# Sixteen experts on one core: tokens of experts 2 to 15 turned by VectorE and SBUF to SBUF transfers instead of TensorE

## The reference

```python
x = x + attention(layernorm(x), context)        # 16 heads of 16, sigmoid scores, no softmax
x = x + ffn(layernorm(x))

def ffn(h):                                     # b=8, s=512, d=256
    logits = einsum('bsd,ed->bse', h, gate_w)
    scores = softmax(logits, axis=-1).transpose(0, 2, 1)
    topk_w, topk_idx = top_k(scores, 64)        # each expert takes 64 tokens of each batch
    x_tok = take_along_axis(h, topk_idx)        # 16 experts x 8 x 64 rows of 256
    g = einsum('becd,efd->becf', x_tok, Wg)     # f = 512
    u = einsum('becd,efd->becf', x_tok, Wu)
    eo = einsum('becf,edf->becd', gelu(g) * u, Wd) * topk_w
    out = scatter_add(zeros, topk_idx, eo)
    shared = (gelu(h @ Ws_g.T) * (h @ Ws_u.T)) @ Ws_d.T
    return out + shared
```

## Time and profile before

| | |
|---|---|
| median of 3 runs | 1411.19 us (1408.72 to 1411.27) |
| the profiled execution, its own time | 1411.32 us |
| its span in the trace | 1409.5 us |
| instructions | 22306 |
| TensorE's granted clock, mean | 0.992 |
| experts, 0 to 15, in the span | from about 1113 us to the end |

### The profile page before, as it was taken

The page is one execution under the profiler, slowest core; times in us unless marked ns, Lnnn a source line. Parts: engine busy times, 40 slices in busy tenths (PEclk is TensorE's granted clock), DMA queues, the critical chain, the costliest instruction groups (busy, mean ns, idle before and its releaser), DMA issues.

```text
span 1409.5 us, 22306 instructions
## 1 busy us (share of the span) xinstructions
PE 1356.8 (96%) x8906; PEld 780.9 (55%) x8906; DVE 647.5 (46%) x1294; ACT 957.5 (68%) x1073; POOL 210.7 (15%) x173
## 2 busy tenths in 40 slices
PE   4869999999999999999999999999999999999997
PEld 3434444444444344444444443324888888888886
DVE  4334245235325424523532531211658777777773
ACT  3556888888887888888888788998232344444442
POOL 1000000000000000000000000020000236666665
PEclk9998999999999999999999999999999999999999
DMA  6482666387378467548737835732433366666644
GB/s 161 127 154 92 126 124 156 112 136 174 109 122 161 136 117 143 148 108 135 190 100 124 163 107 81 138 121 82 174 120 120 120 194 150 150 149 150 150 105 46
DMA packets 97160, 185.82 MB, mean 132 GB/s; under 512 B 16992, under 2 KB 51296, under 8 KB 97056
## 3 DMA queue, kind: packets, MB, share of 16 engines
q1 hardware_dynamic: 80768, 154.08, 46.2%
q0 software_dynamic: 16000, 29.91, 10.3%
q10 hardware_dynamic: 288, 0.39, 0.2%
HBM read 118.99 MB, written 61.83 MB: 128 GB/s over the span
## 4 chain that ended last, share of the span: by engine, by line
PE 87%; ACT 4%; DVE 3%; DMA 2%; issue 2%; SPq 1%; POOL 0%; POOLq 0%; DVEq 0%
PE acc L1318 24%; PE score L1356 18%; PE score L1294 17%; PE score L1371 9%; PE misc L1209 6%; PE misc L1222 6%; ACT probs L683 4%; PE misc L1245 2%; PE misc L1230 2%; PE misc L1237 1%; DMA key_scr<-key_parts 1%; PE misc L1253 1%; DVE o_sum L863 1%; SPq L391 1%; PE acc L1397 1%
## 5 line engine op out<-in xcount | busy, mean ns | idle before, releaser
L683 ACT ACTIVATE probs<-score 128x1024 f32<-128x1024 f32 (+1 forms) x832 | 789.5, 1043 | 166.8 <-PE score L1294 161.9
L1318 PE MATMUL acc<-probs,values 128*32 128x512 f32 (+1 forms) x3328 | 411.9, 601 | 4.5 <-DVE o_sum L863 3.3
L1294 PE MATMUL score<-queries,keys 48*128 48x512 f32 (+1 forms) x1664 | 315.4, 452 | 4.0 <-DMA keys<-key_parts 3.0
L1294 PEld LDWEIGHTS score<-queries,keys 48*128 48x128 f32 (+1 forms) x1664 | 128.4, 181 | 258.7 <-ACT probs L683 200.6
L692 ACT ACTIVATE gelu<-score 128x512 f32<-128x512 f32 x96 | 57.1, 594 | 198.6 <-PE score L1356 198.5
L1318 PEld LDWEIGHTS acc<-probs,values 128*32 128x32 f32 (+1 forms) x3328 | 83.2, 109 | 184.0 <-issue 144.2
L580 POOL DMA_DIRECT2D ctx_raw<-ctx_t x32 | 23.4, 731 | 759.5 <-DVE ctx_lo L771 758.6
L782 DVE CAST key_parts<-misc 128x512 fp32r<-128x512 f32 (+1 forms) x63 | 36.2, 574 | 209.1 <-PE misc L1209 196.0
L1356 PE MATMUL score<-tok_hi,gu_hi 128*128 128x512 f32 x384 | 119.2, 392 | 0.0
L1356 PE MATMUL score<-tok_lo,gu_hi 128*128 128x512 f32 x384 | 118.6, 390 | 0.0
L1356 PE MATMUL score<-tok_hi,gu_lo 128*128 128x512 f32 x384 | 118.5, 390 | 0.0
(11 more groups left out here) (179 smaller groups left out, 1388.8 us busy)
## 6 DMA issues: line engine op xcount, KB each, us to landing
keys<-key_scr SPq DMA_DIRECT2D x180, 200.2 KB, 8.1
key_scr<-key_parts SPq DMA_DIRECT2D x45, 512.0 KB, 4.5
gu_raw<-w_gu SPq DMA_DIRECT2D x17, 1024.0 KB, 6.5
ctx_raw<-ctx_t POOLq DMA_DIRECT2D x24, 512.0 KB, 4.1
queries<-query_scr SPq DMA_DIRECT2D x180, 64.0 KB, 2.8
d_raw<-w_d SPq DMA_DIRECT2D x17, 512.0 KB, 8.7
query_scr<-query_parts SPq DMA_DIRECT2D x15, 512.0 KB, 5.0
xn<-x SPq DMA_DIRECT2D x8, 512.0 KB, 3.8
```

The lines of the kernel that those rows point to most:

```text
L683: act.activation(probs[0:rows, n % RING, 2 * pair:2 * pair + 2, :], score[k % 3][0:rows, :, :], ACT.Sigmoid, scale=SCALE).then_inc(probs_d ...
L1294: mm = pe.matmul(score[k % 3][0:rows, g, :], keys[quarter % KEY_RING][of, pair, P * st:P * st + rows], queries[half][of, e, pair, :], star ...
L1318: mm = pe.matmul(acc[32 * c:32 * (c + 1), :], values[b % 2][0:rows, st, half, c, :], probs[0:rows, n % RING, c, :], start=(st == 0), stop= ...
```

## The change

The rows of experts 2 to 15 no longer go through TensorE. (`DIRECT_ROWS = 2` experts stay as they were.)

1. `turn(e)` on VectorE: one transpose of the gathered rows in blocks of 32 x 32, into `blocks`, a view of the tile `xn`, which the experts otherwise don't use.
2. `place(e)` on SP: the 16 pairs of a block row and a block column are moved to their partitions by 16 transfers of 32 partitions x 2 x 128 elements, into `tok_raw`, a view of the tile `norm`.
3. `turned_tokens(e)` on VectorE: splits `tok_raw` into `tok_hi` and `tok_lo`, two casts and two subtractions, reading in runs of 32 elements.
4. The multiplication by `add_w` moves from VectorE to ScalarE (`expert_result`), between its two pairs of quarters. VectorE keeps the two small copies (`expert_rows`). For the last expert there is one result and one signal per tile of 128 rows, as before.
5. The orders: gathers are issued up to five experts ahead instead of three, the row lists (`rows_of`) four ahead instead of two, the weight load of set e+3 stands ahead of `place(e+2)` on SP, and weight set 3 and `place(2)` ahead of the store of the last shared result.

```diff
             for n in range(1, B + 1):
 
+                if n == B:
+                    sp.wait_ge(set_split, 4)
+                    load_weights(3, 1)
+                    place(2)
...
+            def place(e):
+
+                sp.wait_ge(turned, e + 1 - DIRECT_ROWS)
+                wait_past(sp, tok_split, e - DIRECT_ROWS)
+                for i in range(BLOCKS):
+                    for j in range(BLOCKS):
+                        sp.dma_start(tok_raw[TURN * j:TURN * (j + 1), :, P * i:P * (i + 1)],
+                                     blocks[TURN * i:TURN * (i + 1), j::BLOCKS, :]).then_inc(placed, 16)
...
-            for s in range(3, SETS):
-                sp.wait_ge(set_split, 2 * s - 2)
-                load_weights(s, s % 2)
+            for e in range(1, E):
+                if e + 3 < SETS:
+                    sp.wait_ge(set_split, 2 * e + 4)
+                    load_weights(e + 3, (e + 1) % 2)
+                if e + 2 < E:
+                    place(e + 2)
...
+                if e >= 2 + DIRECT_ROWS:
+                    pool.wait_ge(turned, e - 1 - DIRECT_ROWS)
+                elif e >= 2:
                     pool.wait_ge(tok_full, TABLES + KC * (e - 1))
...
+            for e in range(5):
+                gather(e, e % 2)
             for e in range(E):
-                if e + 3 < E:
-                    gather(e + 3, (e + 1) % 2, True)
+                if e + 5 < E:
+                    gather(e + 5, (e + 1) % 2)
                 add_rows(e, e % 2)
...
+            def expert_result(e, par):
+                act.wait_ge(adds_ready, 2 * e + 1)
+                for t in range(TT):
...
+                    act.wait_ge(d_full, 2 * (e + B) + t // 2 + 1)
+                    last = act.activation(result[par][:, t, :], d_bank[:, t // 2, D * (t % 2):D * (t % 2 + 1)],
+                                          ACT.Copy, scale=add_w[par][:, t:t + 1])
+                    if t % 2:
+                        last.then_inc(scaled, 1)
...
                 if more_sets:
                     hi_parts(0, par, e + 2, n - 1)
+                if e:
+                    expert_result(e - 1, 1 - par)
                 gelus(n, (2, 3))
...
+            def turn(e):
+
+                par = e % 2
+                dve.wait_ge(rows_in[par], 8 * TT * (e - par) + 16 * TT)
+                wait_past(dve, placed, PLACE_DMAS * (e - DIRECT_ROWS))
+                dve.transpose(blocks.rearrange("p j (t q) -> p t j q", q=TURN),
+                              gathered[par][:].rearrange("p t (j q) -> p t j q", q=TURN)).then_inc(turned, 1)
+
+            def turned_tokens(e):
+                par = e % 2
+                dve.wait_ge(placed, PLACE_DMAS * (e + 1 - DIRECT_ROWS))
+                for k in range(KC):
+                    raw = tok_raw[:, k, :].rearrange("p (i t q) -> p t i q", i=BLOCKS, q=TURN)
+                    hi = tok_hi[par][:, k, :].rearrange("p (t i q) -> p t i q", i=BLOCKS, q=TURN)
+                    lo = tok_lo[par][:, k, :].rearrange("p (t i q) -> p t i q", i=BLOCKS, q=TURN)
+                    dve.tensor_copy(hi, raw).then_inc(tok_step, ts.up())
+                    dve.wait_ge(tok_step, ts.now())
+                    last = dve.tensor_tensor(lo, raw, hi.bitcast(F32), ALU.subtract)
+                last.then_inc(tok_split, 1)
...
                 hidden_quarters(n, par, (0, 1))
-                if more_tokens:
+                if e + 1 < DIRECT_ROWS:
                     tokens(1 - par)
+                    rows_of(e + 3, 1 - par, True)
+                elif e + 1 < E:
+                    turned_tokens(e + 1)
+                if e + 2 < E:
+                    turn(e + 2)
+                if e + 4 < E:
+                    rows_of(e + 4, par, True)
+                if e + 1 < E:
                     set_lo(0, par, e + 2)
-                if more_rows:
-                    rows_of(e + 2, par, True)
                 if e == 0:
                     shared_result(B - 1)
                 else:
-                    expert_result(e - 1, 1 - par)
+                    expert_rows(e - 1, 1 - par)
                 hidden_quarters(n, par, (2, 3))
```

More of the change, by code:

```diff
@@ L40 @@
 STACK_DMAS = 16 * 2 * len(KEY_PART)
+TURN = 32
+BLOCKS = P // TURN
+PLACE_DMAS = 16 * BLOCKS ** 2
+DIRECT_ROWS = 2
 E, F, CAP = 16, 512, 64
@@ L271, in build @@
             logits = sb("logits", [P, TT, B, E])
+        blocks = xn[:].rearrange("p t d -> p (t d)").rearrange("p (j c) -> p j c", c=P)
+        tok_raw = norm[:].rearrange("p t d -> p (t d)").rearrange("p (k s) -> p k s", s=S)
         last_out = logits[0:E].rearrange("p t b e -> p (t b e)")
@@ L336, in build @@
         d_copied = sem("d_copied")
+        scaled = sem("scaled")
         tok_full = sem("tok_full")
         tok_copied = sem("tok_copied")
+        turned = sem("turned")
+        placed = sem("placed")
         tok_step = sem("tok_step")
+        tok_split = sem("tok_split")
         soft_step = sem("soft_step")
@@ L732, in _ @@
                     hi_parts(1, 1, 1, None)
+            def expert_result(e, par):
+                act.wait_ge(adds_ready, 2 * e + 1)
+                for t in range(TT):
+                    if e + 1 == E:
+                        act.wait_ge(d_full, 2 * (e + B) + t + 1)
+                        act.activation(result[par][:, t, :], last_bank[t], ACT.Copy, scale=add_w[par][:, t:t + 1]
+                                       ).then_inc(scaled, 1)
+                        continue
+                    act.wait_ge(d_full, 2 * (e + B) + t // 2 + 1)
[3 more added lines that the diff above has]
+                        last.then_inc(scaled, 1)
             def expert(e, par, more_sets):
@@ L746, in _ @@
                 expert(e, e % 2, e + 2 <= E)
+            expert_result(E - 1, 1)
         @block.vector
@@ L1028, in expert_result @@
                                 ).then_inc(adds_ready, 1)
[L1029 to L1037, removed]
-                                             d_bank[:, t // 2, D * (t % 2):D * (t % 2 + 1)],
-                                             add_w[par][:, t:t + 1], None, ALU.mult)
-                    if t % 2:
-                        last.then_inc(d_copied, 1)
             def rows_of(e, par, before):
@@ L1170, in _ @@
                     tokens(0)
+                    rows_of(2, 0, True)
                     set_lo(0, 1, 1)
@@ L1190, in expert @@
                 else:
-                    expert_result(e - 1, 1 - par)
+                    expert_rows(e - 1, 1 - par)
                 hidden_quarters(n, par, (2, 3))
-                if more_tokens:
+                if e + 1 < E:
                     set_lo(1, par, e + 2)
             for e in range(E):
-                expert(e, e % 2, e + 1 < E, e + 2 < E)
-            expert_result(E - 1, 1)
+                expert(e, e % 2)
+            expert_rows(E - 1, 1)
         @block.tensor
@@ L1444, in _, with expert @@
                 up(n, par, 0, (2, 3))
-            def expert(e, par, more):
+            def expert(e, par):
                 n, slot = e + B, 1 - par
                 pe.wait_ge(set_split, 2 * e + 3)
-                pe.wait_ge(tok_copied, TABLES + KC * e + KC)
+                if e < DIRECT_ROWS:
+                    pe.wait_ge(tok_copied, TABLES + KC * e + KC)
+                else:
+                    pe.wait_ge(tok_split, e + 1 - DIRECT_ROWS)
                 up(n, par, slot, (0, 1))
-                if more:
+                if e + 1 < DIRECT_ROWS:
                     transpose_rows(e + 1, 1 - par)
@@ L1457, in _ @@
             for e in range(E):
-                tf.n = TABLES + KC * e + KC
-                expert(e, e % 2, e + 1 < E)
+                expert(e, e % 2)
             pe.wait_ge(set_split, 2 * SETS)
```

20 lines of the change are left out of this document (9 added, 11 removed).

## The result

| | before | after |
|---|---|---|
| median | 1410.07 us (1408.72 to 1411.27, 4 runs) | **1395.67 us** (1395.58 to 1397.41, 4 runs) |
| profiled execution, its span | 1411.32, 1409.5 | 1395.58, 1393.7 |

What follows compares the result with a forecast made beforehand. TensorE (PE), busy 96% of the span, was taken as the bound. Removing 12.2, 0.75 and 0.1 us, together 13.05, from 1411.32 gave 1398.3; the median of runs, 0.13 lower, 1398.1 us, range 1397.1 to 1408.5.

Steps and rivals of the forecast that it cites:

- What is removed: PE's transposes in experts 2 to 15, 12.2 us, and 0.75 us at expert 1, all on the path.
- The tail's 0.1 us: After the last products, the result on ACT instead of DVE: about 380 ns against 0.50 us, 0.1 us less.
- VectorE: Per expert on DVE: split 2.1 us, transpose 1.2, sum about 12.1 of 16.67 us.
- ScalarE's slack: ACT's third gelu, queued behind four results until T+15.3 (T: expert's first up product); PE needs its bank at T+16.67: 1.4 us.
- The ring: Loop from turn through 16 transfers and split to the next turn: 15.1 us, 16.3 with slow landing, against PE's 16.67.
- The DMA engines: Busy time per expert with the 16 added transfers, 0.27 us each: 15.5 of 16.67 us, nearly full.
- POOL: Four gathers and four adds per expert: 13.3 of 16.67 us; the new casts might add up to 0.8.
- The sum: Whole kernel: 13.05 us off the profiled 1411.32, giving 1398.3 us, if nothing new waits.
- the lower end of the range: Whole kernel: 1397.1 us, if the end or start of the experts gives another microsecond.
- A: Transfer loop in the experts somewhat too long, 17.0 to 17.4 us: 2.9 to 8.1 us lost, 1401.0 to 1406.2; chance 0.26.
- B: Transfer loop in the experts becomes the bound at 18.3 us, above the old 17.54: 1417.9 us, slower; chance 0.13.
- C: Transfer loop in the experts near the old period, 17.6 to 17.95 us: nothing gained, 1408.5 to 1414; chance 0.06.

Runs made afterwards that it cites:

- run 2: The changed kernel once more, unchanged: 1398.75 us, ratio 0.9907 to the kernel before.
- Run 6: The changed kernel with four of its 16 transfers per expert cut into two, 20 in all, same bytes: 1423.56 us, ratio 1.0107.
- run 8: The changed kernel with two buffers each for turned blocks and placed rows, split behind gu_lo, and expert 1's rows also turned by VectorE: 1399.33 us, ratio 0.9924.
- run 10: The changed kernel again, unchanged, side by side with a version with two buffers each: 1397.32 us, ratio 0.9919.
- Run 9: The changed kernel with only 4 of the 16 transfers per expert, the other 12 left out: 1395.99 us, ratio 0.9913.

## Why the prediction was right, and where it failed

- **What is removed.** "14 x 0.87 = 12.2 us, all of it on the path", and 0.75 us at expert 1: 12.95. Measured between fixed points of two traces: 13.08. Right. With the 0.3 us that the end of the program costs more, the change is worth some 12.8 us; in the medians it was 14.4 us in the result and 12.3 us in run 2.
- **The tail's 0.1 us.** Wrong. The step was ScalarE's 256-wide read of PSUM at 380 ns, taken from 593 ns at 512 by the slope of operations of 1024 to 2048 elements that read SBUF. It took 475 ns, so the last result is 0.48 instead of 0.50 us. The slope itself was right: ScalarE's reads of PSUM have a median of 598 ns at 512 elements and 1025 at 1024, 0.83 ns per element too. What the step left out is the scale that is read for each partition (`add_w`), which the gelu doesn't have. The 256-wide operation of this kernel with two such operands, a scale and a bias (`xn<-xn,rs_mean,rs`), has a median of 586 ns, where 632 ns at 512 (`hid_hi`) less the slope gives 419: an estimated 0.08 us for each. One of them makes the 380 ns 464, close to the 475. No run isolates it.
- **VectorE.** Split 2.23 (2.1), transpose 1.24 (1.2), sum 12.19 us (12.1). Right. The estimate from the Trainium skill's "VectorE: DVE Perf Modes" for the transpose, 1.2 us, is confirmed by this row. The advice in the Trainium skill, "VectorE: DVE Perf Modes", "Rules for kernel authors", to use TensorE for a 128x128 transpose, was decided by the measurement the other way: TensorE is the engine that has no time, and 13 us were gained. Run 6, with a ring longer than the old period, and run 8 are the cases here in which TensorE was the better place.
- **ScalarE's slack** of 1.4 us: 1.3. Right, with the chain of run 2 showing it used up, there by a late gelu and not by late rows.
- **The ring** of 15.1 us, 16.3 at worst: 15.84 by run 6's arithmetic, a median of 15.6 us by the events of the result's trace. So the 15.1 was 0.5 to 0.7 low: the mean pitch of a group is 0.66 instead of 0.63 (15 x 0.03 = 0.4), the split 2.23 for 2.1 and the landing 2.3 for 2.2 (0.1 each). The worst case was too low: the landing reached 3.8 us in the result's trace and 5.0 in run 10, where 3.4 was the bound, and single turns took 16.9 and 18.1 us. The forecast held all the same: the long turns are few, and the slack behind them, which the prediction lets be used up once, is there again after the next short turn.
- **The DMA engines** at 15.5 of 16.67: 12.8. Too high. A transfer of 64 packets of 512 B was set equal to one of 32 of 2 KB. Run 9 gives it directly: the share falls from 0.73 (run 10) to 0.63 for twelve transfers fewer, 0.10 x 16.66 / 12 = 0.14 us of each engine per transfer, not 0.27.
- **POOL** at 13.3 us: 12.06 by the window. Held with room. The 0.8 us that the two casts of the split might have added did not come: the adds that lie beside the split alone took 1.57 to 1.68 us, where 1.55 is usual. A slow gather, which the prediction doesn't have, came in their place (last section).
- **The sum**: 1398.3 against the profiled execution. The experts' part of the gain was right to 0.1 us, and pooled over the result and runs 2 and 10 the changed kernel's 16 executions have a median of 1397.3 us (1395.4 to 1400.9), within the range, though by 0.2 us only.
- **The step that failed is the lower end of the range**, "1397.1, if the end or the start of the experts gives another microsecond". It allowed for an error of the sum alone, and put the part ahead of the experts at no change without a reason; in the result's trace that part was 3.0 us shorter. The range had no term for the spread of executions, though the three times shown already lay 2.6 us apart, and the part ahead of the first fixed point moves by up to 4.6 us between traces (1116.31 to 1120.89). A lower end at 1398.1 less the 2.6 between the times shown, 1395.5, would have held the result. What was wrong is the range, not the mechanism.
- **The rivals.** A: its mechanism occurs in single executions, for 0.6 us in run 10. B: not here; its case was met with four more transfers (1.0107). C: is the kernel with 18 transfers (0.9983), give or take half a microsecond.

What stays open: what at the start of attention makes an execution 1 or 4 us longer, what held PE back in run 8, what delays PE's signals in run 2, and the 0.3 us at the very end.

## What to carry to other kernels

Work taken from the bounding engine comes off the end in full, provided the loop it is moved into, buffer by buffer and queue by queue, is shorter than the new period; add that loop up from its rows first, test its margin by lengthening it, and look at its single turns, since the mean hides the long ones. A wait in the changed kernel is not yet the new work's: follow it back to the first engine that was late. A queue that issues small SBUF to SBUF transfers is paid by the issue (here 0.65 us each, for 16 KB as for 32 KB), so the number of transfers is the size to watch. And the range of a forecast needs a term for the spread of executions, even where the work outside the change is the same.

## What the runs showed of the hardware beyond the forecast

The first gather of each group on POOL is slow when it lies beside VectorE's gu_lo, which reads two SBUF operands:

```profile
1222.85 2.30 POOL L657 DMA_INDIRECT gathered<-norm_scr,gather_row  x1 [2.45 <-DVE gather_row L1081]
1225.46 0.98 POOL L657 DMA_INDIRECT gathered<-norm_scr,gather_row  x1 [0.31 <-ACT result L774]
```

It takes 2.30 us, and the ones outside 0.95 to 0.98; gu_lo runs from 1221.98 to 1224.26 (first fence on VectorE), so the gather ends 0.9 us behind it, about the length of a whole gather. The result's trace has 13 gathers that start within gu_lo, and all of them end 0.82 to 0.91 us behind its end, wherever in it they start: one that starts 0.82 us after gu_lo takes 2.28 us, one that starts 1.24 us after it 1.90. The one that starts in the same moment as gu_lo took 0.94 us, as the gathers of the kernel before do (0.94 to 1.02) where no operation with two SBUF inputs lies beside them. So a gather that comes second waits until gu_lo has ended. This is read from the places in the traces; no run changed it on purpose. The second finding is the pitch of SP's queue: a median of 0.64 us from issue to issue for 32 KB and 16 KB transfers alike (run 6). The third is run 8: pauses of PE of 0.2 to 0.45 us that wait for nothing shown. The fourth is run 2: signals of PE that reach ScalarE up to 2.3 us later than usual, while PE itself goes on.
